# Row halves for the 64-row products of neighbouring chunks in the experts' first layer, and an output projection in float32

## What is computed

```python
# attention, e = 192
out = einsum('bhqk,bhkd->bhqd', softmax(masked scores), v)      # 6 heads of 32
t = t + (out.reshape(b, s, e) @ Wo + bo)
# experts, DIM = 192, HID = 768, 4 experts
n = layernorm(t)
probs = softmax(n @ gate_w + gate_b)          # the two best kept, scaled to sum 1
h = gelu(einsum('bsd,edh->ebsh', n, w1) + b1)
y = einsum('ebsh,ehd->ebsd', h, w2) + b2
t = t + einsum('bse,ebsd->bsd', kept, y)
```

## Time and profile before

| | before |
|---|---|
| median of the timed runs | 1730.26 us |
| profiled execution | 1726.64 us |
| its span | 1724.8 us |
| TensorE busy | 1581.2 us (92%) |
| VectorE busy | 1211.1 us (70%) |
| ScalarE busy | 932.3 us (54%) |
| GpSimd busy | 234.4 us (14%) |

### The profile page before, as it was taken

How to read it: one execution, slowest core, us unless ns; L and a number is a source line. 1 busy time by engine, 2 the same in 40 slices (tenths; PEclk the granted TensorE clock), 3 DMA queues, 4 the chain that set the end, 5 groups by cost and what they waited for, 6 DMA issues and landing times.

```text
span 1724.8 us, 32985 instructions
## 1 busy us (share of the span) xinstructions
PE 1581.2 (92%) x13264; PEld 1018.6 (59%) x13264; DVE 1211.1 (70%) x2544; ACT 932.3 (54%) x1378; POOL 234.4 (14%) x296
## 2 busy tenths in 40 slices
PE   1579999899999999999999999999999999999998
PEld 0334576556765566655765557654666556765666
DVE  6776875857867676767758587676776777686743
ACT  2315655366544765456553665537654566536664
POOL 3021112011020112001030110201111010301100
PEclk9668999999999999999999999999999999999999
DMA  4221002010020001010020100201001100200000
GB/s 128 97 55 38 1 1 65 1 48 1 1 65 29 20 1 46 20 48 1 2 65 1 47 2 1 65 1 47 1 22 45 47 2 2 64 2 11 1 10 10
DMA packets 25102, 48.19 MB, mean 28 GB/s; under 512 B 7411, under 2 KB 16819, under 8 KB 23573
## 3 DMA queue, kind: packets, MB, share of 16 engines
q1 hardware_dynamic: 15840, 28.63, 6.1%
q0 software_dynamic: 6144, 9.45, 2.3%
q10 hardware_dynamic: 2966, 8.01, 1.3%
HBM read 20.70 MB, written 6.29 MB: 16 GB/s over the span
## 4 chain that ended last, share of the span: by engine, by line
PE 64%; DVE 25%; ACT 5%; issue 3%; DMA 1%; POOL 1%; SPq 0%; DVEq 0%; ACTq 0%
PE ps L429 20%; PE ps L707 16%; PE ps L654 8%; DVE mx L1157 7%; PE ps L464 5%; PE ps L588 4%; DVE acc L1313 3%; DVE room L1329 3%; PE ps L508 2%; DVE u L1027 2%; PE ps L436 1%; DVE norm_stats L998 1%; PE ps L495 1%; ACT room L870 1%; DVE gn_st L1040 1%
## 5 line engine op out<-in xcount | busy, mean ns | idle before, releaser
L870 ACT ACTIVATE room<-ps,b_sb 128x512 f32<-128x512 f32 x384 | 263.2, 686 | 461.9 <-PE ps L429 460.7
L707 PE MATMUL ps<-wout_h,room 128*128 128x192 f16 x3072 | 462.4, 247 | 5.4 <-DVE acc L1313 5.4
L1329 DVE SCALAR_TENSOR_TENSOR room<-room 128x512 f16<-128x512 f32 x384 | 263.6, 690 | 177.8 <-ACT room L876 172.8
L707 PE MATMUL ps<-wout_l,room 128*128 128x192 f16 x1536 | 379.4, 247 | 0.0
L707 PEld LDWEIGHTS ps<-wout_h,room 128*128 128x128 f16 x3072 | 287.8, 98 | 46.0 <-DVE acc L1313 11.8
L848 ACT ACTIVATE room<-ps 128x1024 f32<-128x1024 f32 (+3 forms) x288 | 225.4, 809 | 143.1 <-PE ps L468 90.8
L1157 DVE TENSOR_REDUCE mx<-ps 128x2 f32<-128x1024 f32 (+3 forms) x288 | 266.3, 953 | 40.4 <-PE ps L592 19.9
L876 ACT ACTIVATE room<-room 128x512 f16<-128x512 f32 x384 | 241.9, 630 | 34.3 <-PE ps L707 0.7
L654 PE MATMUL ps<-room,v 128*64 128x512 f32 (+3 forms) x1152 | 232.6, 488 | 0.0
L588 PE MATMUL ps<-qk 96*128 96x512 f16 (+3 forms) x576 | 160.6, 352 | 37.6 <-DVE mx L1157 28.2
L464 PE MATMUL ps<-qk 98*64 98x512 f16 (+3 forms) x1152 | 157.2, 333 | 11.7 <-DVE mx L1157 7.8
(11 more groups left out here) (210 smaller groups left out, 2382.3 us busy)
## 6 DMA issues: line engine op xcount, KB each, us to landing
xc<-x_ch SPq DMA_DIRECT2D x8, 768.0 KB, 6.0
qk<-qk_all SPq DMA_DIRECT2D x96, 64.0 KB, 2.5
qk<-qk_all POOLq DMA_DIRECT2D x96, 64.0 KB, 2.5
out<-acc ACTq DMA_DIRECT2D x16, 384.0 KB, 2.5
xt<-x_tok SPq DMA_DIRECT2D x7, 768.0 KB, 7.3
qk<-qk_all POOLq DMA_DIRECT2D x96, 32.0 KB, 2.0
qk<-qk_all SPq DMA_DIRECT2D x96, 32.0 KB, 2.3
room<-w_in SPq DMA_DIRECT2D x2, 1024.0 KB, 10.6
```

Source lines behind the costliest of these rows:

```text
L707: mm = pe.matmul(dst, hid[:, s, tok], w[:, n, :], start=(k == 0 and m == 0 and t % 2 == 0), stop=False, skip_group_check=True)
L870: act.activation(h32[:, i % N_H, :], ps[:, H_BANK[i], :], ACT.Gelu, scale=1 / (U_SCALE * W_SCALE), bias=b1_sb[:, n:n + 1])\
L1329: V.scalar_tensor_tensor(out=h_l[:, s, :], in0=h32[:, s, :], scalar=A_SCALE, in1=h_h[:, s, :], op0=ALU.mult, op1=ALU.subtract)\
```

## The change

In `hidden`, the product of `win_t` with `ul` now uses only the high rows of the weight; the low part times the low part is left out. The changed kernel copies the high 64 rows of `w1` once into `w1_two`, even chunks in partitions 0 to 63 and odd chunks in 64 to 127 (two DMAs at the start). In an even chunk, after its four full products, TensorE makes two products of 64 rows: one on rows 0 to 63 that ends this chunk's bank, and one on rows 64 to 127 that begins the bank of the next chunk. The odd chunk then has four products. The wait for the next chunk's bank moves to a place inside the even chunk.

The projection takes `o32` as it is, in float32, against `wo32`: two products for each token tile. `o_h`, `o_l`, ScalarE's copies and GpSimd's subtractions go. `o32` has its own buffer, for one block at a time, so VectorE waits for `wo_ps` before it writes the first pair of a block. The due times of block 0's tail are 1.5 items earlier, which is one item at each place.

```diff
-TAIL_AT = ({"wo": 20, "residual": 20, "norm": 24, "turn": 27, "high": 28, "low": 28, "scores": 31,
-            "gate": 31, "best": 33},
+TAIL_AT = ({"wo": 18.5, "residual": 18.5, "norm": 22.5, "turn": 25.5, "high": 26.5, "low": 26.5, "scores": 29.5,
+            "gate": 29.5, "best": 31.5},
...
+        w1_two = sb("w1_two", [P, CHUNKS // 2, P], F16)
+        wo32 = sb("wo32", [P, 2, C], F32)
-        o32 = tmp[:, 0:2 * N].rearrange("p (c n) -> p c n", c=2)
+        o32 = sb("o32", [P, 2, QB], F32)
...
+            sp.wait_ge(stage_hi, sum(kind != "out" for kind, _, _ in pieces))
+            for odd in range(2):
+                chunks = win_t[0:TAIL, COL_W1:].rearrange("p (k two n) -> p k two n", two=2, n=P)[:, :, odd, :]
+                sp.dma_start(w1_two[odd * TAIL:(odd + 1) * TAIL, :, :], chunks).then_inc(w1_two_in, 16)
...
-                pe.wait_ge(o_hi, at(o_hi, img, (b + 1) * PAIRS))
-                pe.wait_ge(o_lo, at(o_lo, img, (b + 1) * PAIRS))
-                for t in range(b * TB, (b + 1) * TB):
...
-                    for n, (lhs, rhs) in enumerate(terms):
...
+                pe.wait_ge(o_done, at(o_done, img, (b + 1) * PAIRS))
+                for t in range(TB):
+                    dst = ps[:, bank + t // 2, (t % 2) * C:(t % 2 + 1) * C]
                     tok = slice(t * P, (t + 1) * P)
+                    pe.matmul(dst, o32[:, 0, tok], wo32[:, 0, :], start=True, stop=False)
+                    mm = pe.matmul(dst, o32[0:TAIL + 1, 1, tok], wo32[0:TAIL + 1, 1, :], start=False, stop=True)
...
+                    even = i % 2 == 0
+                    if even:
+                        bank_free(i)
...
+                    for k, (w, a, c) in enumerate(((win_h, uh, 0), (win_l, uh, 0), (win_h, ul, 0), (win_t, uh, 1))):
+                        mm = pe.matmul(ps[:, H_BANK[i], :], w[:, cols], a[:, c, tok],
+                                       start=(even and k == 0), stop=(not even and k == 3))
+                    if even:
+                        bank_free(i + 1)
+                        mm = pe.matmul(ps[:, H_BANK[i], :], w1_two[0:TAIL, n // 2, :], ul[0:TAIL, 1, tok],
+                                       start=False, stop=True)
+                    mm.then_inc(h_ps, 1)
+                    if even:
+                        pe.matmul(ps[:, H_BANK[i + 1], :], w1_two[TAIL:P, n // 2, :], ul[TAIL:P, 1, tok],
+                                  start=True, stop=False)
...
-            def high_of_output(img, run):
...
-                def low_of_output(run):
...
+                        if pair == 0 and (b or later):
+                            dve.wait_ge(wo_ps, at(wo_ps, img, b * TB // 2))
-                            ins = V.tensor_tensor(o32[h * D:(h + 1) * D, pair // 2, b * QB:(b + 1) * QB],
+                            ins = V.tensor_tensor(o32[h * D:(h + 1) * D, pair // 2, :],
```

More of the change, by code:

```diff
@@ L672, in experts, with bank_free @@
             def experts(img, following):
-                def hidden(i):
-                    b, n = divmod(i, CHUNKS)
+                def bank_free(i):
                     if i == 0:
@@ L803, in front @@
                 rows_of_maxima(img, 0, 4)
-            def high_of_output(img, run):
-                b, pair = divmod(run, PAIRS)
-                act.wait_ge(o_done, at(o_done, img, run + 1))
-                rows = slice(2 * D * (pair % 2), 2 * D * (pair % 2) + 2 * D)
-                act.activation(o_h[rows, pair // 2, b * QB:(b + 1) * QB],
-                               o32[rows, pair // 2, b * QB:(b + 1) * QB], ACT.Copy)\
-                   .then_inc(o_hi, 1)
             def store(img, b):
@@ L835, in attend @@
                 aside = Aside(tail(img, 0))
-                ends = run_ends()
-                run = 0
                 for j, (b, pair, kc) in enumerate(E_ITEMS):
@@ L853, in attend @@
                         rows_of_maxima(img, 1, 3)
-                    if run < len(ends) and j == ends[run] + 6:
-                        high_of_output(img, run)
-                        run += 1
                     aside.until(j)
                 aside.finish()
-                assert run == len(ends) - 1
             def experts(img, following):
@@ L953, in attend @@
                 spread_keys(img)
-                def low_of_output(run):
-                    b, pair = divmod(run, PAIRS)
-                    if run:
-                        pool.wait_ge(o_lo, at(o_lo, img, run))
-                    pool.wait_ge(o_hi, at(o_hi, img, run + 1))
-                    rows = slice(2 * D * (pair % 2), 2 * D * (pair % 2) + 2 * D)
-                    where = (rows, pair // 2, slice(b * QB, (b + 1) * QB))
-                    nc.gpsimd.tensor_tensor(o_l[where], o32[where], o_h[where], ALU.subtract).then_inc(o_lo, 1)
                 def power_of_tail(b):
@@ L968, in power_of_tail @@
                       .then_inc(pow2_done, 1)
-                for run in range(NB * PAIRS):
-                    low_of_output(run)
-                    if run == PAIRS - 1:
-                        power_of_tail(0)
-                pool.wait_ge(o_lo, at(o_lo, img, NB * PAIRS))
+                power_of_tail(0)
+                pool.wait_ge(pow2_done, at(pow2_done, img, 1))
                 power_of_tail(1)
```

45 lines of the change are left out of this document (17 added, 28 removed).

## The result

The change made the kernel slower: 1739.93 us median (1738.46 to 1741.61, 10 runs) against 1732.69 (1725.88 to 1737.41, 10 runs) of before on the same chip, ratio 1.0039 with a 95% interval of 1.002 to 1.0058. The profiled executions lie further apart, 1739.06 against 1726.64 us, spans 1737.2 and 1724.8. The forecast was 1730, no change. The loss is small, but its interval leaves out 1.

A forecast was written before the change was run, and what follows sets the result against it. TensorE was taken to set the pace (64% of the chain of waits); +3.8 + 9.3 - 9.9 - 2.4 + 1.6 = +2.4 on the profiled 1726.64 gave 1729.0, raised towards the timed median to 1730 us; range 1698 to 1752.

The forecast's parts named there:

- the projection: Attention's output projection in float32: 2.58 us a block against 2.00, +9.3 us over 16 blocks.
- the shift: Block 0's tail earlier: transposes' wait for `u` goes, -9.9 us, and 0.3 us an image behind exponentials, -2.4.
- the price of a pair: Experts' two neighbouring chunks: side-by-side halves plus entering and leaving the mode take 0.45 us against 0.43, +3.8 us over 192 pairs.
- my test was 2.16: Experts: the forecast is wrong if hidden products of a pair of chunks together last other than 2.16 us.
- Halves in turn: Rival in the experts: halves run one after the other, 0.66 us a pair, TensorE +44 us, 1762 us; chance 0.13.
- free edges: Rival in the experts: row halves enter and leave without a gap, 41 us less on TensorE, 1700 us; chance 0.22.
- The saving and the two edges cancel.: Experts' pairs: 0.215 us for the halves plus both edges is 0.45 us against 0.43, +3.8 us.
- my own rival: Free mode changes in the experts: a third of pairs precede VectorE waits, so 30 us gained, 1700 us; chance 0.22.
- the start of the experts: First chunks: the other bank is asked for one slot earlier, so TensorE waits longer for attention's last output, +1.6 us.
- All of it lies on TensorE between its own products: Output projection: the added 0.58 us a block counts in full, +9.3 us over 16 blocks.
- transposes and exponentials: Block 0's tail in attention: wait for `u` gone, -9.9 us; 0.3 us an image behind exponentials gone, -2.4 us.

The follow-up runs named there:

- e3_tail_only: The kernel before with only the earlier due times of block 0's tail (f16 projection, five full products in each chunk): 1713.59 us, ratio 0.9884 to before.
- e2_no_pairs: The changed kernel with the experts' five full products of each chunk back, float32 projection and earlier tail kept: 1713.05 us, ratio 0.9884 to before.
- e4_one_full: The changed kernel with one full 128-row product into the even chunk's bank in place of the two halves: 1711.19 us, ratio 0.9867 to before.
- e9: The changed kernel with pairs beginning at odd chunks, plus four more products ahead of the row-maxima waits in chunks 39 and 45: 1710.4 us.
- e10: The changed kernel with pairs beginning at odd chunks, plus two more products ahead of the row-maxima waits in chunks 39 and 45: 1706.59 us.
- e12: The kernel before with four more full products ahead of the row-maxima waits in chunks 39 and 45: 1722.04 us, ratio 0.9928 to before.
- e11: The changed kernel without pairs, plus seven more full products in chunk 0 of every image: 1735.44 us, ratio 1.0003 to before.
- e7: The changed kernel with four more full products in each of chunks 38 and 44 of each image: 1740.77 us, ratio 1.0039 to before.
- e13: The changed kernel with the due times of block 0's tail as in the kernel before: 1739.88 us, ratio 1.0032 to before.
- e8: The changed kernel with eight more full products once, at the start of the experts of image 3: 1738.97 us, ratio 1.0028 to before.
- e5: The changed kernel with two full 128-row products in the places of the two halves: 1739.61 us, ratio 1.0039 to before.

## Why the prediction was wrong

Two steps failed: the sum had no term for TensorE's clock, and it took saving and cost of a pair as one term. A third, the projection, was priced too high. Taken one after the other (before, e3_tail_only, e2_no_pairs, after) and without the stretches, the shift gave -10.4 us, the projection +2.0 and the pairs +9.5, together +1.1, where I had -12.3, +9.3 and +5.4, together +2.4. That the total of these is right is luck. The stretches added 12.0 between the profiled executions.

**Right: the price of a pair.** Edges of 0.10 and 0.107 us and halves side by side, 0.425 against my 0.45 and the 0.43 of before, with the edges taken from the column halves. The Trainium skill ("TensorEngine Tiling (Array Packing)", Key Properties) says that a change of tiling mode drains the engine; for row halves the trace now agrees, at 0.1 us a side. Hidden products of a pair in after take 2.14 us, my test was 2.16. Halves in turn and free edges are both out. e4_one_full gives 28.7 us for free edges, near my 30.

**Failed: "The saving and the two edges cancel."** They cancel in TensorE's time, but not in the order. I had booked saving and cost as one term, when they stand in different chunks: cost in the even one, always paid, saving in the odd one, ahead of the waits for an expert's sum, of those of chunks 17, 25 and 27 and of the long waits of the row maxima. In my own rival I let a third of a saving drown in such waits, and did not ask it of the forecast. In an image six waits grow by 0.21 and one shrinks by it (the chunks are named in the section on the result): 5 x 0.21 = 1.05, and with 0.11 at the start of the experts nearly all of the 1.17 us that the pairs cost in an image without a stretch. Only one of these waits is for an expert's sum. In the last image six are, and from its first hidden product to the end it takes 114.53 us in e2_no_pairs and 115.86 in after, 1.33 more. In all 7 x 1.17 + 1.33 = 9.5 us, where I had 3.8 + 1.6.

**Failed: the clock was not in the sum.** The page's strip showed it full, and I asked no windows of the row maxima. There before already has four stretches at 1.2 GHz, each behind waits for the maxima. The pairs lengthen exactly these waits by 0.2 us (chunk 39: 1.29 to 1.51, chunk 45: 1.66 to 1.87), and the profiled execution of after has 7 stretches more, +12.0 of its +12.4 us. That filling the waits takes the stretches away is shown three times (e9, e10, e12). That length is not all is shown too: equal waits had 0, 1, 4 and 6 stretches (e2, e3, before, e11), and 1.5 and 1.87 us had 3, 8, 9, 10 and 11 (e7, e13, e4, e8, after and e5). With waits of 1.29 and 1.66 us an image of 201.2 us has next to none, one of 202.5 several. No run lengthens the waits and leaves the image as it is, so that the added 0.2 us are what brings the pairs' stretches is likely, and not shown. The distance of repeated stretches is that of two images (409.6 us in after, 406.2 before), and one image shifted in time lost its stretch. What exactly the chip looks at is left open.

**Failed in size: the projection.** Its own time is as forecast. Block 0's in the first image of after, to be read beside the earlier trace rows:

```profile
163.43 0.49 PE L619 MATMUL ps<-wo,o 65*128 65x192 f32 x2
163.76 0.49 PE L618 MATMUL ps<-wo,o 128*128 128x192 f32 x2
164.09 0.49 PE L619 MATMUL ps<-wo,o 65*128 65x192 f32 x2
```

Two passes stand 0.33 us apart, so a block takes 16 x 0.163 = 2.61 us against 2.00; the attention has 0.63 more. But block 1's stands ahead of TensorE's wait for `gn_v`, which VectorE sets; before and after, TensorE there:

```profile
813.28 0.33 PE L483 MATMUL ps<-gn_v,kst 96*96 96x2 f32 x2 [1.58 <-DVE gn_v L1057]
```
```profile
816.92 0.33 PE L487 MATMUL ps<-gn_v,kst 96*96 96x2 f32 x2 [0.52 <-DVE gn_v L1043]
```

One microsecond of cover that I did not look for. It hides block 1's 0.6 us in seven of eight images. The wait even shrinks by 1.17 us in e2_no_pairs (1.75 to 0.58), which makes the experts 0.52 shorter; why it is more than 0.6 was not separated. In all the projection costs some 2 us (7 x 0.10, 0.63 in the first attention, 0.64 in the last experts) instead of 9.3. The step that failed here is "All of it lies on TensorE between its own products".

**Right in kind: transposes and exponentials.** I had -12.3 us for the shift; alone it gives 1.30 an image, -10.4 over eight attentions. Beside the float32 projection it gives only 0.51 an image (e13_old_tail), which I had not asked. In the changed kernel, as forecast, the refinement stands ahead of the normalization and the transposes follow TensorE's work without a wait (answers to the earlier trace rows). VectorE and TensorE there:

```profile
991.65 0.29 DVE L1016 COPY u<-u 128x256 f32<-128x256 f32 x1
991.86 1.38 DVE L1275 TENSOR_TENSOR o<-ps,tmp 32x512 f32<-32x512 f32 x2
```
```profile
992.58 1.02 PE L651 MATMUL ps<-room,v 128*64 128x512 f32 x4
993.53 1.09 PE L440 MATMUL ps<-kst,u 128*128 128x128 f32 x8
```

**Right: the start of the experts**, a longer wait for the last output (0.53 to 0.75 us), 0.11 us an image where I had 0.2.

**The base.** I set the forecast by the profiled execution of before. Over the batches its timed runs went from 1725.88 to 1740.35 us. In those measured beside the experiments the mean granted clock falls from 0.974 (1726.06 us) to 0.965 (1740.35 us), 1.6 us for each 0.001. One stretch, 3.4 us at half clock in 1730, lowers the mean by 0.001 and costs about 1.6 us. So stretches account for the whole spread, and from the 4 of the profiled execution (0.973) I estimate 3 to 12 in those runs, seven or eight in the middle ones (0.969 to 0.970). The ten runs of after have 0.965 to 0.967, by the same estimate 10 to 12. The profiled execution of before was thus a lucky one. In the medians after has some three or four stretches more, 5 to 6 us of the 7.2, where the two profiled executions differ by 7 stretches and 12.4 us.

## What to carry to other kernels

When two costs cancel, ask where each stands in the order: ahead of a wait on another engine a saving turned into idle time here, and a cost was hidden, so the same pair moved by one chunk went from 1.2 us an image lost to 0.7 gained. Waits that repeat in one place (here 1.1 to 1.9 us) can bring TensorE down to 1.2 GHz for some 3 us; look for it with short windows, not in the page's strip, and fill the wait with work that fits (in e10_odd_fill2 two products that leave the result unchanged, in each of two waits). Fill behind the products that the other engine waits for, not ahead of them (e7_fill), compare several executions and not two profiles where the clock moves, and read cover again for each combination of edits, since two edits may be hidden by the same wait.

## What I had not expected of the hardware

- Two 64-row halves in row mode start together and take the time of one product (0.215 us for 512 columns), with 0.10 us idle on the way in and 0.107 on the way out.
- Whether there are stretches at 1.2 GHz depends on the length of an image, at equal waits (e11_none_longer: none to six for 1.34 us more an image), and where they repeat they do so at a constant distance (409.6 us in after).
- Executions of one kernel, unchanged, differ by 14 us (before, 1726 to 1740) in step with the mean granted clock (0.974 to 0.965).
